# Layer 1's remainders: one GpSimd subtraction and one DMA transpose for a tile, in place of two halves of each

## What is computed

```
h = einsum('bnc,hdc->bhnd', x, Wh)                 # 8 x 4 instances of 2048 x 64
scores = where(mask, einsum('...nd,...md->...nm', h, h), NEG)
attn = softmax(scores, axis=-1)
out_h = einsum('...nm,...md->...nd', attn, h) + bh
...                                                # leaky relu, Wo, a second pass with one head
```

## Time and profile before

| what | us |
|---|---|
| median of the runs | 3323.97 (3322.51 to 3327.71, three runs) |
| the profiled execution | 3323.41 |
| its span, first to last instruction | 3321.7 |
| layer 1, about 320 to 2430 of the span | 2110 |

### The profile page before, as it was taken

How to read it: one execution, slowest core, us unless ns; L and a number is a source line. 1 busy time by engine, 2 the same in 40 slices (tenths; PEclk the granted TensorE clock), 3 DMA queues, 4 the chain that set the end, 5 groups by cost and what they waited for, 6 DMA issues and landing times. The chain is left out here.

```text
span 3321.7 us, 126248 instructions
## 1 busy us (share of the span) xinstructions
PE 3065.0 (92%) x49399; PEld 2287.0 (69%) x49399; DVE 2739.8 (82%) x5344; ACT 2369.3 (71%) x2806; POOL 2546.0 (77%) x1861
## 2 busy tenths in 40 slices
PE   5856799999999999999999999999986699999997
PEld 3425577777777777777777777777765577777775
DVE  6664688888888888888888888888877599898998
ACT  1146677777777777777777777777766588787886
POOL 1136598989999999899999999999976257676775
PEclk8979999999999999999999999999998899999998
DMA  5207889998899889999988998899867433332321
GB/s 207 67 1 271 223 156 153 165 161 163 155 164 169 157 156 173 159 159 161 167 164 155 163 166 165 154 166 166 163 122 235 165 124 134 119 130 115 132 116 73
DMA packets 1189166, 507.67 MB, mean 153 GB/s; under 512 B 1090718, under 2 KB 1148508, under 8 KB 1186588
## 3 DMA queue, kind: packets, MB, share of 16 engines
q1 hardware_dynamic: 1187564, 497.60, 70.8%
q0 software_dynamic: 1200, 3.93, 0.3%
HBM read 102.12 MB, written 62.91 MB: 50 GB/s over the span
## 5 line engine op out<-in xcount | busy, mean ns | idle before, releaser
L633 POOL TENSOR_TENSOR mask_slot<-probs 128x1024 f16<-128x1024 f32 x1024 | 1916.1, 1893 | 221.8 <-ACT probs L1017 138.4
L1017 ACT ACTIVATE probs<-scores,shifted_max 128x2048 f32<-128x2048 f32 x512 | 1026.1, 2004 | 166.6 <-DVE shifted_max L1222 159.0
L1217 DVE CUSTOM_DVE_ANT_0 scores<-ps,mask 128x1024 f32<-128x1024 f32 x512 | 625.5, 1222 | 202.4 <-PE ps L860 196.5
L859 PE MATMUL ps<-operands 128*128 128x512 f16 x2048 | 777.3, 380 | 1.7 <-DVE neg_max L1217 1.7
L860 PE MATMUL ps<-operands 128*128 128x512 f16 x2048 | 776.7, 379 | 0.0
L1022 ACT COPY probsT<-ps 128x1024 bf16<-128x1024 bf16 x512 | 518.0, 1012 | 359.3 <-PE ps L868 359.3
L1217 DVE CUSTOM_DVE_ANT_0 scores<-ps,mask,neg_max 128x1024 f32<-128x1024 f32 x512 | 657.3, 1284 | 103.4 <-issue 57.7
L868 PEld LDWEIGHTS ps<-ident,probs 128*128 128x128 bf16 x8192 | 519.6, 98 | 294.7 <-issue 160.7
L868 PE MATMUL ps<-ident,probs 128*128 128x128 bf16 x8192 | 624.2, 219 | 8.3 <-issue 3.7
L879 PE MATMUL ps<-v_parts,probsT 128*128 128x64 f16 x8192 | 547.6, 193 | 0.0
L878 PE MATMUL ps<-v_parts,probsT 128*128 128x64 f16 x8192 | 547.2, 193 | 0.0
(11 more groups left out here) (175 smaller groups left out, 4575.1 us busy)
## 6 DMA issues: line engine op xcount, KB each, us to landing
mask_slot<-mask SPq DMA_DIRECT2D x129, 512.0 KB, 2.9
operands<-hT_d SPq DMA_DIRECT2D x40, 512.0 KB, 4.1
operands<-hT_d SPq DMA_DIRECT2D x80, 256.0 KB, 4.6
v_parts<-h_d SPq DMA_DIRECT2D x40, 512.0 KB, 4.6
scores<-in_adj SPq DMA_DIRECT2D x16, 1024.0 KB, 4.8
h_d<-probs SPq DMA_DIRECT2D x32, 512.0 KB, 3.5
hT_d<-probs SPq DMA_DIRECT2D x32, 512.0 KB, 2.8
probsT<-mask_slot SPq DMA_TRANSPOSE x1024, 3.6
```

The source lines that it names most:

```text
L633: pool.tensor_tensor(low[:, u, w], probs[:, u, w], high[:, u, w], ALU.subtract).then_inc(sem(f"low{half}"), 1)
L859: pe.matmul(ps[:, b, :], hi_lo[:, p, t * P:(t + 1) * P], hi_lo[:, p, w], start=True, stop=False)
L1017: act.activation(probs[:, 1 - u, :], scores[:, 1 - u, :], ACT.Exp, bias=shifted_max[:, 1 - u:2 - u], scale=-1.0, accum_out=row_sum[:, held ...
L1217: dve.tensor_tensor_reduce(scores[:, u, w], ps[:, 2 * c:2 * c + 2, :].rearrange("p a n -> p (a n)"), mask[:, t * N + c * 2 * BANK:t * N + ...
```

## The change

POOL makes the remainders of a tile in one operation of 2048 columns instead of two of 1024, and SP moves them in one DMA transpose instead of two. The semaphores of the halves become one for the subtraction (`low`) and one for each slot of the transpose (`low_turned0`, `low_turned1`). PE waits once, ahead of its first product, instead of ahead of the first and the ninth.

```diff
             def layer1_step(g, i, t, p, back):
                 u = t % 2
-                for half in range(2):
-                    if back(2):
-                        sp.wait_ge(sem(f"low{half}"), g - 1)
-                        gate(sp, "sp")
-                        if half == 0:
-                            since(sp, sem("weighed"), g - 3)
-                            gate(sp, "sp")
-                        w = slice(half * N // 2, (half + 1) * N // 2)
-                        sp.dma_start_transpose(lowT[:, u, w].rearrange("p (c q) -> p c q", q=P), low[:, u, w]).then_inc(sem(f"low_turned{half}{u}"), 16)
+                if back(2):
+                    sp.wait_ge(sem("low"), g - 1)
+                    gate(sp, "sp")
+                    since(sp, sem("weighed"), g - 3)
+                    gate(sp, "sp")
+                    sp.dma_start_transpose(lowT[:, u, :].rearrange("p (c q) -> p c q", q=P), low[:, u, :]).then_inc(sem(f"low_turned{u}"), 16)
...
-                    for half in range(2):
-                        if back(3):
-                            pool.wait_ge(sem(f"low_turned{half}{u}"), turns(g - 3, u))
-                            gate(pool, "pool")
-                        w = slice(half * N // 2, (half + 1) * N // 2)
-                        pool.tensor_tensor(low[:, u, w], probs[:, u, w], high[:, u, w], ALU.subtract).then_inc(sem(f"low{half}"), 1)
+                    if back(3):
+                        pool.wait_ge(sem(f"low_turned{u}"), turns(g - 3, u))
+                        gate(pool, "pool")
+                    pool.tensor_tensor(low[:, u, :], probs[:, u, :], high[:, u, :], ALU.subtract).then_inc(sem("low"), 1)
...
-                        if c % 8 == 0:
-                            pe.wait_ge(sem(f"low_turned{c // 8}{u}"), turns(g - 4, u))
+                        if c == 0:
+                            pe.wait_ge(sem(f"low_turned{u}"), turns(g - 4, u))
...
-                    since(act, sem("low1"), g - 2)
+                    since(act, sem("low"), g - 2)
```

More of the change, by code:

```diff
@@ L532, in _ @@
             for u in range(2):
-                for half in range(2):
-                    sp.wait_ge(sem(f"low_turned{half}{u}"), turns(LAYER1 * NT - 2 + u, u))
+                sp.wait_ge(sem(f"low_turned{u}"), turns(LAYER1 * NT - 2 + u, u))
             load_z(0, 1)
```

## The result

The changed kernel takes 3364.76 us (median of 4 runs, 3362.61 to 3365.36), the kernel before in the same measurement 3323.24 us. The ratio is 1.0121, 95% interval 1.0103 to 1.0139: slower by 41 us, where 143 were forecast. The direction was right, the size was 3.5 times too large.

The account below looks back on a forecast made before the run. PE was taken as the bound, busy 3065.0 of 3321.7 us. Late landings cost 0.31 us per step, 0.28 after some comes back; 512 x 0.28 = 143 us on 3323.4 gives 3467 us, 8-in-10 range 3320 to 3650.

Parts of the forecast that it names:

- the merged one takes L + 0.9: Transpose of the remainders: one whole lands 0.9 us later after issue than a half, for its additional data.
- L: Time from issue to landing of a half's transpose before the change: least 2.7 us, median 3.7, most 6.7.
- The loop: POOL's slot over two steps: subtraction, issue, landing, restart sum to 4.75 us plus a half's landing time, against 8.21.
- Half of the loops late by 1.24 us: POOL's slot wait: landings above the median make it late, 0.62 us for two steps, 0.31 for one.
- Some comes back: POOL's 0.54 us of room per step and PE's 1.8 us at the least landing reduce 0.31 to 0.28 us.
- 4.7 as the stand-in for the upper half: Half-transpose landings between 3.7 and 6.7 us were represented by 4.7, making their two-step slot cycle 9.45 us.
- some 200 us or more: Sign in the changed profile: POOL's idle time released by the DMA ahead of its subtraction, where it was 61.8 us.
- 100 us or more: Sign in the changed profile: PE's products with the turned remainders wait this long for the landing.
- the step of 4.38: Sign in the changed profile: one step of layer 1 takes 4.38 us, where it took 4.10.
- Issue before data: Rival: merged transpose moves nothing until a 2.46 us issue ends; 3757 us, or some 3650; chance 0.14.
- Absorbed: Rival: slack takes all of POOL's lateness, as late tiles may be followed by early ones; 3324 us, chance 0.13.
- Faster: Rival: one landing per tile meets disturbance once, so PE's 11.2 us of waits go; 3311 us, chance 0.05.

Follow-up runs that it names:

- four slots: Four slots for the remainders instead of two: under the changed kernel 3333.41 us, under the kernel before (halves) 3315.31 us.
- early wait: The kernel before, but a tile's first subtraction waits for both landings of two tiles before; 3329.11 us, ratio 1.0021.
- shorter subtraction: The changed kernel with 1536 of 2048 columns subtracted, the other remainders left at zero, the whole still transposed; 3322.10 us, ratio 1.0005.
- changed, short loads: The changed kernel with layer 1's four operand loads moving 16 partitions each instead of 128 or 64; 3333.25 us, ratio 1.0048.
- halves with short loads: The kernel before with layer 1's four operand loads moving 16 partitions each instead of 128 or 64; 3309.39 us, ratio 0.9968.

## Why the prediction was right in direction and wrong in size

**The bound.** Right for the kernel before: PE sets its pace, and the loss can be read as PE's wait at one line. In the changed kernel POOL is no longer behind ACT but behind its own loop: 68% of its subtractions, 500 to 2400, start as soon as their slot's landing lets them.

**The subtraction.** Forecast 3.53 to 3.60 us, 3.56 taken; measured 3.602. The f32 forms with a fixed part of 189 ns were the nearer ones: 2 x 1.893 - 0.189 = 3.597.

**The transpose.** The step that failed first is "the merged one takes L + 0.9", applied to the whole distribution of L. It holds for the least landing (2.7 to 3.6) and neither for the median (3.7 to 3.8, forecast 4.6) nor for the mean (3.79 to 4.22). The runs divide this. Where POOL kept its timing by ACT, with four slots, the mean was 4.44 us for wholes and 3.81 for halves: 0.63 more, and not 0.9. Its transposes:

```profile
L491 SPq DMA_TRANSPOSE probsT<-mask_slot x232: 1557/1644/4552, 500.2 to 2397.6; - x116
...
DMA to landing us min/median/max: 3.6/4.2/6.8
```

The median there, 4.2 us, includes the slower slot `spare`; out of `mask_slot` alone it is 4.0. Another 0.2 came off the mean where POOL started behind a landing, as 0.1 did with the early wait alone. I read it so: of two halves in one step, a disturbed one delays the other too, and both delays were in the L that I took; a whole meets the disturbance once. In the trace of before, the landing times of a tile's two halves do go together (correlation 0.49 from 500 to 2400), but that one delays the other was argued, not shown. Shown is that the mean lies 1.1 us above the least landing for halves, 0.8 for wholes at the same timing, and 0.6 for wholes behind a waiting POOL.

**The loop.** The mechanism was right: the longer loop lost 257 us, four slots gave back most of the loss and a shorter subtraction all of it. The loops of six kernels, from a tile's first subtraction to the moment when its slot is free again, as the mean over 500 to 2400, stand in line with their loss:

| kernel | mean loop, us | slower by, us |
|---|---|---|
| shorter subtraction | 7.35 | 2 |
| early wait, nothing merged | 7.75 | 8 |
| changed, short loads | 8.03 | 24 (over halves with short loads) |
| changed | 8.18 | 41 |
| two subtractions, one transpose | 8.25 | 53 |
| one subtraction, two transposes | 9.00 | 257 |

Two steps of before are 8.21 us. In the changed kernel 34% of the loops are longer than that, where the forecast had half. From the subtraction's end to the issue it is 0.20 us in the mean, where the prediction's one tile had 0.09. Of the lateness that is left, part stays with POOL: it waited 266.8 us for landings and worked 0.16 us less in each step, and the step grew by 0.07 us.

**The sum.** Two terms were mis-sized. "Half of the loops late by 1.24 us", 0.31 us per step, was a third of the loops late by 0.87 us: 0.15 per step. "Some comes back" took 0.31 down to 0.28; measured, 0.15 became 0.07, so half came back and not a tenth. What the prediction lists as slack, POOL's room in a step and PE's room at the tile, may be what gave it back; how much each gave no run divides. Had every landing grown by 0.9 us, the trace's own landings of before would give 0.25 to 0.30 us per step by the prediction's rule, so 4.7 as the stand-in for the upper half was not the fault. What turned up as forecast was POOL's wait for the DMA ("some 200 us or more": 266.8). What did not: PE's wait of "100 us or more" (35.2 at the products from 500 to 2400, 47.5 over the whole span) and the step of 4.38 (2146.2 / 512 = 4.19).

**What lengthens a landing.** The loads of operands carry about 17 of the 41 us. The instruction DMA and the output's store were in every run, so their share of the other 24 us stays open. The trace of the changed kernel narrows it. Of 452 transposes, 71 had neither a packet of the instruction DMA nor a load or store in flight between issue and landing: they landed after 3.7 us in the mean and 4.1 at the most, and none of their loops was late. Of the 155 late loops, 136 had such a packet in flight. A longer landing also meets more packets, so this is a hint and not a share.

**The rivals.** *Issue before data* is out: SP is held for 1.63 us and data moves before that ends. *Absorbed* was nearer than the forecast (41 us from its 3324, where 3467 is 102 away), but not by its cause alone: slack took half of the lateness, and the rest of the difference is lateness that never arose. *Faster* named what may be a true part, that a disturbance hits a whole once where it hits two halves twice; it was no gain because the clean landing is 0.9 us later. Its condition, "L + 0.9 under 4.4", was a slip: by the prediction's own 9.05 - 3.56 - 0.09 the bound is 5.4, as its passage on PE's wait has it (L over 4.5). The rule of the Trainium skill that it cites (DMA: Bandwidth & Descriptors, section Bandwidth, on batching) stands under measurements of transfers from HBM to SBUF that GpSimd issued. These transposes go from SBUF to SBUF and are issued by SP, and no run here isolates what that rule names. The time lay inside the range of 3320 to 3650, but that range was wide, and 3467 was far off.

**Splitting a transfer.** The Trainium skill (Perfetto Trace Analysis, section DMA Optimizations) says that splitting DMAs may let some start sooner, and the whole end sooner if the DMA engines are generally idle. The runs agree where the first half does start sooner. With four slots, where POOL waits for no slot, the halves are at a ratio of 0.9990 and the whole at 1.0043: 18 us. Where both halves were issued behind one subtraction, neither started sooner than a whole would, and the kernel was the slower one, at 1.0784. The engines were idle only between transfers, though: over 500 to 2400 they were busy for 90.7% before and 77.0% after.

## What to carry to other kernels

Before merging two transfers out of a double-buffered slot, add up the slot's loop (work, issue, landing, restart) and compare it with the number of slots times the step. Use the mean landing and its tail, not the median: the changed kernel's loop looked 0.5 us short of the limit by its median and stood at it by its mean. In this kernel a mean loop 0.9 us under the limit cost nothing that could be told, one at the limit 41 us, and one 0.8 us over it 257. A spread of landing times is not a constant to be shifted by the added data; here the least landing grew by the whole 0.9 us and the mean by half of that. If the merge is wanted for other reasons, more slots bought most of it back here.

## What was not expected of the hardware

- One DMA transpose of 128 x 2048 two-byte elements held SP for 1.63 us, one of 128 x 1024 for 1.24: the second 1024 columns cost a third of the first.
- The DMA engines' busy share in layer 1, 500 to 2400, fell with the merge from 90.7% to 77.0% for nearly the same bytes per tile. The queue rows of before and after:

```profile
q1 hardware_dynamic: 993505, 303.31, 90.7%
```

```profile
q1 hardware_dynamic: 962018, 297.82, 77.0%
```

- Two transposes issued back to back behind one subtraction landed with a median of 2.9 us each (mean 3.38), against 3.7 (3.79) when they were issued half a step apart.
